# A perceiver's wide cross attention: order of TensorE's work in every second step, and of ScalarE's and VectorE's beside it

## What is computed

```python
def _L0_xattn_ref(x, context, ln_gamma, ln_beta, w_q, w_kv, w_out, b_out, gate):
    xn = _layernorm(x, ln_gamma, ln_beta)
    q = (xn @ w_q).reshape(B, SQ, NUM_HEADS, DIM_HEAD)
    kv = context @ w_kv
    k, v = jnp.split(kv, 2, axis=-1)
    k = k.reshape(B, SK, NUM_HEADS, DIM_HEAD)
    v = v.reshape(B, SK, NUM_HEADS, DIM_HEAD)
    scores = jnp.einsum('bqhd,bkhd->bhqk', q * SCALE, k)
    attn = jax.nn.softmax(scores, axis=-1)
    out = jnp.einsum('bhqk,bkhd->bqhd', attn, v).reshape(B, SQ, INNER)
    out = out @ w_out + b_out
    return out * jnp.tanh(gate[0])
```

## Time and profile before

| | |
|---|---|
| median of 3 runs | 4327.76 us (4327.47 to 4329.01) |
| the profiled execution | 4329.77 us |
| its span, first to last instruction | 4327.1 us |
| TensorE busy with matmuls | 3896.4 us (90% of the span) |
| VectorE, ScalarE, POOL busy | 2700.6, 2460.7, 1633.4 us |
| mean granted TensorE clock | 0.952 of full speed |
| DMA, mean over the span | 168 GB/s |

### The profile page before, as it was taken

How to read it: one execution, slowest core, us unless ns; L and a number is a source line. 1 busy time by engine, 2 the same in 40 slices (tenths; PEclk the granted TensorE clock), 3 DMA queues, 4 the chain that set the end, 5 groups by cost and what they waited for, 6 DMA issues and landing times. The chain is left out here.

```text
span 4327.1 us, 75594 instructions
## 1 busy us (share of the span) xinstructions
PE 3896.4 (90%) x27192; PEld 2768.8 (64%) x27192; DVE 2700.6 (62%) x4077; ACT 2460.7 (57%) x4518; POOL 1633.4 (38%) x1301
## 2 busy tenths in 40 slices
PE   5899999999999999999677985899999999967399
PEld 2677777777777777776445974555555555433288
DVE  5766666666666666664174213677777777658577
ACT  3577777777777777776142112455555556625165
POOL 1566666666666666666222002100000000014033
PEclk9999999999999999999797997999999999979699
DMA  5777777776777766663213566644444422100011
GB/s 200 269 253 250 245 255 253 250 255 240 265 252 250 247 238 224 228 226 118 65 20 120 197 230 209 191 147 138 143 147 140 137 69 66 34 23 1 12 50 42
DMA packets 232719, 724.99 MB, mean 168 GB/s; under 512 B 44556, under 2 KB 129804, under 8 KB 163724
## 3 DMA queue, kind: packets, MB, share of 16 engines
q1 hardware_dynamic: 229664, 711.78, 48.3%
q0 software_dynamic: 2688, 8.39, 0.5%
HBM read 625.70 MB, written 94.37 MB: 166 GB/s over the span
## 5 line engine op out<-in xcount | busy, mean ns | idle before, releaser
L752 POOL TENSOR_TENSOR wa_acc<-wa_acc,wa_probs 128x512 f32<-128x512 f32 x960 | 1246.4, 1298 | 526.8 <-ACT wa_probs L613 446.4
L677 DVE TENSOR_REDUCE wa_mx<-wa_ps_m 128x2 f32<-128x1024 f32 x512 | 626.8, 1224 | 486.5 <-PE wa_ps_m L488 486.3
L613 ACT ACTIVATE wa_probs<-wa_ps_s 128x512 f32<-128x512 f32 x1024 | 556.0, 595 | 528.9 <-PE wa_ps_s L534 523.6
L1204 ACT ACTIVATE na_probs<-na_ps_s 128x512 f32<-128x512 f32 x1024 | 564.2, 599 | 379.1 <-PE na_ps_s L1108 373.7
L1256 DVE TENSOR_REDUCE na_mx<-na_ps_m 128x1 f32<-128x512 f32 x1024 | 643.5, 682 | 187.7 <-PE na_ps_m L1093 186.7
L605 ACT ACTIVATE wa_ps_s<-wa_m_wide 128x512 f32<-128x512 f32 x1024 | 575.4, 605 | 1.0
L510 PE MATMUL wa_ps_o<-wa_probs,wa_values 128*64 128x256 f32 x4096 | 507.3, 390 | 0.0
L1093 PE MATMUL na_ps_m<-na_keys,na_q 98*128 98x512 f32 x1024 | 425.1, 423 | 43.6 <-DVE na_mx L1256 30.2
L1108 PE MATMUL na_ps_s<-na_q,na_keys 100*128 100x512 f32 x1024 | 430.4, 428 | 2.4 <-ACT na_probs L1204 1.5
L449 PE MATMUL wa_ps_k<-wa_k_ctx,wa_w_k 128*128 128x512 f32 x1488 | 388.3, 396 | 0.0
L475 PE MATMUL wa_ps_v<-wa_w_v,wa_v_ctx 128*128 128x256 f32 x2880 | 383.1, 282 | 0.0
(11 more groups left out here) (342 smaller groups left out, 5503.6 us busy)
## 6 DMA issues: line engine op xcount, KB each, us to landing
wa_k_ctx<-ctx_split SPq DMA_DIRECT2D x248, 1024.0 KB, 5.1
wa_v_ctx<-ctx_split SPq DMA_DIRECT2D x120, 1024.0 KB, 5.8
na_ctx<-ctx_split SPq DMA_DIRECT2D x56, 1024.0 KB, 6.9
na_keys<-k_rows SPq DMA_DIRECT2D x192, 256.0 KB
ctx_split<-wa_stage SPq DMA_DIRECT2D x32, 1024.0 KB, 9.1
wa_land<-in_ctxT SPq DMA_DIRECT2D x32, 512.0 KB, 9.9
ge_w_b<-in_w_rows SPq DMA_DIRECT2D x8, 2048.0 KB
k_rows<-na_k_high SPq DMA_DIRECT2D x64, 256.0 KB, 2.3
```

What stands on the lines that cost most here:

```text
L613: act.activation(probs[:, c % R:c % R + 2, h * SQ:(h + 1) * SQ], ps_s[n % BANKS][:, :].rearrange("p (c n) -> p c n", c=2), ACT.Exp).then_i ...
L677: dve.tensor_reduce(mx[:, half, :, k], ps_m[:, :, :], AX.X, ALU.max).then_inc(m_taken, 1)
L752: pool.tensor_tensor(acc[:, :], acc[:, :], probs[:, c % R, :], ALU.add).then_inc(summed, 1)
L1204: act.activation(probs[:, n % RP, :], ps_s[n % RS][:, :], ACT.Exp).then_inc(exp_done, 1)
```

## The change

In odd steps TensorE keeps its order. In even steps the value unit comes first, then the high products, which now open the sum, then the maximum, then the low products, which now close it and tell ScalarE of it (s_ready, one increment a head). The low products of an even step thus stand right before the weighing of the odd step behind. On ScalarE initial(2t+3) moves between the two exponentials, except at st 15. On VectorE the rest of the keys goes before the maximum.

```diff
@@ -518,22 +518,29 @@
                                     start=True, stop=True)
                 ins.then_inc(den_done, 1)
 
-            def scores(t):
+            def seeded(t):
+                if t % ST == 0:
+                    pe.wait_ge(kl_ready, 2 * CG * (t // ST + 1))
+                pe.wait_ge(init_done, 2 * t + 2)
+
+            def scores_low(t, last):
                 a, c = t // ST, t % ST * 2
-                n = 2 * t
-                if c == 0:
-                    pe.wait_ge(kl_ready, 2 * CG * (a + 1))
-                pe.wait_ge(init_done, n + 2)
                 for i in range(2):
                     for h in range(2):
                         r = slice(h * DH, (h + 1) * DH)
-                        pe.matmul(ps_s[(n + h) % BANKS][:, i * SQ:(i + 1) * SQ], keys[a % 2][h][r, (c + i) * P:(c + i + 1) * P],
-                                  ql[a % 3][r, :], start=False, stop=False, skip_group_check=True)
+                        ins = pe.matmul(ps_s[(2 * t + h) % BANKS][:, i * SQ:(i + 1) * SQ], keys[a % 2][h][r, (c + i) * P:(c + i + 1) * P],
+                                        ql[a % 3][r, :], start=False, stop=last, skip_group_check=True)
+                        if last and i:
+                            ins.then_inc(s_ready, 1)
+
+            def scores_high(t, last):
+                a, c = t // ST, t % ST * 2
                 for h in range(2):
                     for i in range(2):
-                        ins = pe.matmul(ps_s[(n + h) % BANKS][:, i * SQ:(i + 1) * SQ], keys[a % 2][h][:, (c + i) * P:(c + i + 1) * P],
-                                        qh[a % 3][:, h, :], start=False, stop=True, skip_group_check=True)
-                    ins.then_inc(s_ready, 1)
+                        ins = pe.matmul(ps_s[(2 * t + h) % BANKS][:, i * SQ:(i + 1) * SQ], keys[a % 2][h][:, (c + i) * P:(c + i + 1) * P],
+                                        qh[a % 3][:, h, :], start=False, stop=last, skip_group_check=True)
+                    if last:
+                        ins.then_inc(s_ready, 1)
 
             open_banks()
             for k in range(CG):
@@ -554,18 +561,29 @@
                 if st == 1 and t > 1:
                     denominator(a - 1)
                 unit = max_unit(t)
-                if t >= -1 and unit is not None:
-                    maximum(*unit)
-                if 0 <= t < LAST:
-                    scores(t)
-                if st == ST - 1 and a + 1 < G:
-                    turn_maximum(a + 1)
-                kb = key_block(t)
-                if kb is not None:
-                    project_keys(kb)
-                unit = value_unit(t)
-                if unit is not None:
-                    project_values(*unit, turns=(t + 1) // ST + 1)
+                values_unit = value_unit(t)
+                if t % 2:
+                    if t >= -1 and unit is not None:
+                        maximum(*unit)
+                    if 0 <= t < LAST:
+                        seeded(t)
+                        scores_low(t, False)
+                        scores_high(t, True)
+                    if st == ST - 1 and a + 1 < G:
+                        turn_maximum(a + 1)
+                    kb = key_block(t)
+                    if kb is not None:
+                        project_keys(kb)
+                if values_unit is not None:
+                    project_values(*values_unit, turns=(t + 1) // ST + 1)
+                if t % 2 == 0:
+                    if 0 <= t < LAST:
+                        seeded(t)
+                        scores_high(t, False)
+                    if t >= -1 and unit is not None:
+                        maximum(*unit)
+                    if 0 <= t < LAST:
+                        scores_low(t, True)
 
         @block.scalar
         def _(act):
@@ -626,16 +644,18 @@
                 kb = key_block(t - 1)
                 if kb is not None:
                     take_keys(kb)
+                ahead = st == ST - 1 and a + 1 < G
                 if t >= 0:
                     exponents(2 * t)
+                    if not ahead:
+                        initial(2 * t + 3)
                     exponents(2 * t + 1)
-                if st == ST - 1 and a + 1 < G:
+                if ahead:
                     take_maximum(a + 1)
                     initial(2 * t + 2)
-                if t >= -1:
                     initial(2 * t + 3)
-                    if st != ST - 2:
-                        initial(2 * t + 4)
+                if t >= -1 and st != ST - 2:
+                    initial(2 * t + 4)
                 if t >= 0 and st == 4 and a < BLOCKS - CG:
                     split(a + CG)
 
@@ -723,14 +743,14 @@
                     take_values(*unit)
                 if st == 1 and t > 1:
                     copy_out(a - 1)
+                kb = key_block(t - 1)
+                if kb is not None:
+                    take_keys(kb)
                 unit = max_unit(t)
                 if t >= -1 and unit is not None:
                     take_maximum(*unit)
                 if st == ST - 2 and 0 <= a < G - 1:
                     finish_maximum(a + 1)
-                kb = key_block(t - 1)
-                if kb is not None:
-                    take_keys(kb)
                 if t == LAST + 1 or (st == 3 and 1 <= a < G):
                     divide(a - 1)
                 if st == 5 and 0 <= a < BLOCKS - CG:
```

## The result

The changed kernel takes 4348.3 us (median of 5 runs, 4344.6 to 4351.0) against 4327.8: ratio 1.0047, 95% interval 1.0036 to 1.0058, so slower by 20 us. The profiled execution took 4349.35 around a span of 4346.7, 19.6 more than before.

The account below looks back on a forecast made before the run. The prediction took TensorE's queue length to bound the main stretch. Its terms, -48.5 + 33.3 + 26.0 + 2.4 + 2.3 - 4.2 + 6.2 - 1 = +16.5, on 4329.8 less 2.0 gave 4344 us, range 4320 to 4368.

Parts of the forecast that it names:

- Regrouping: TensorE's step pairs: four changes of array shape instead of five, 0.19 us saved in each of 255 pairs, -48.5.
- Two value units: Steps 43 to 46: the second value unit waits for VectorE's copy out of ps_v, 1.11 us each, +33.3.
- Keys before the maximum: Pairs without a value unit: VectorE's later maximum stalls TensorE 1.18 us, 22 times, +26.0.
- The steps of the splits: Where ScalarE also splits context, the chain to the next maximum misses by some 0.10 us, 23 times, +2.3.
- free by 0.4: Regular pairs: VectorE's maximum ends at 6.72 us, the next wants to start at 7.11, so no wait.
- Block edges: Low's wait for initial goes at 15 edges with values, -4.2 us; high waits longer at 15 without, +6.2.
- The last block: Earlier initial(2t+3) is worth 0.34 us each, but POOL's sums already take 5.57 a pair: -1 (0 to -3).
- A: Rival, faster: TensorE's change from low to weighing is free, another 38 us goes, 4306; chance 0.10.
- B: Rival, about the same: waits of terms 2 and 3 are 0.3 us shorter, 52 times, 4328; chance 0.15.
- D: Rival, slower: TensorE's change from low to weighing costs 0.20 us or more, +13, 4357; chance 0.05.
- E: Rival: no gain from grouping, as full-array matmuls' loads cannot run under the one before, 4392 us; chance 0.02.
- C: Rival, slower: the clock falls in the first block's pairs and some double-value pairs, 4354 to 4384 us; chance 0.12.

Follow-up runs that it names:

- e5: Changed kernel with ScalarE's and VectorE's orders as before, only TensorE's order changed; ratio 1.0162 to the kernel before, span 4398.8 us.
- e2: Changed kernel with TensorE projecting values before keys in odd steps that have a value unit; ratio 0.9975 to the kernel before, span 4317.5 us.
- e1: Changed kernel with the maximum before the keys on VectorE in even steps without a value unit; ratio 0.9989 to the kernel before, span 4318.5 us.
- e6: Changed kernel with TensorE's order as before, only ScalarE's and VectorE's orders changed; ratio 1.0074 to the kernel before, span 4359.1 us.
- e4: Changed kernel with ScalarE's order as before, both exponentials and then both initials; ratio 1.0062 to the kernel before, span 4347.1 us.
- e8: Changed kernel with the edits of e1 and e2, and the division's product moved from step 3 to step 7; ratio 0.9909, span 4287.3 us.
- e9: As e8, with TensorE's old order in step 0 of blocks without a value unit there; ratio 0.9908 to the kernel before, span 4288.3 us.
- e3: Changed kernel with VectorE's division in step 4, behind the maximum, instead of step 3; ratio 1.0134 to the kernel before, span 4378.6 us.

## Why the prediction was right, point by point

The forecast was 4344 with a range of 4320 to 4368 and "slower" at 0.67; measured are 4348.3.

1. *Regrouping* (-48.5): 0.200 a regular pair instead of 0.19, low to weighing 0.15 as taken. e5 shows that it comes from TensorE's order alone. No price of the second increment shows.
2. *Two value units* (+33.3): the wait is 0.92 net of the saving in 30 pairs, as forecast; e2 took it away and got 31.8 back.
3. *Keys before the maximum* (+26.0): the mechanism was right, and e1 and e6 show it; the size was 1.32 a wait instead of 1.18, because ScalarE's initial starts 0.09 behind the exponential that it waits for, not 0.03, twice before the keys. e4, without these waits, has it at some 0.6 (TensorE idle 0.53). It fell on 21 of the 22 pairs; the earliest waits only some 0.3.
   *The steps of the splits* (+2.3) failed. What made the next maximum late in the changed kernel is the division, in 30 pairs and by 0.33, 7 more than forecast. The step that failed is one that the forecast doesn't name: VectorE's division stands in front of the keys at step 3 and was put at nothing. With the product at its 0.47 of before it might have passed; on the new order it meets POOL's sum and takes 1.09. Odd blocks lost the delay in e1, where the product takes 0.43 again, even blocks in e8, where it is moved away. The room was also smaller than the forecast's "free by 0.4": with the 0.65 that it takes from a waiting maximum it is 0.25, which is why it could have the splits miss by 0.10. The split's own price is 0.25 and not 0.10; it shows in e1 in 12 odd blocks and in e8 in 11 even ones too, the 23 of the forecast, and is hidden behind the division's wait in the changed kernel.
4. *Block edges* (-4.2 and +6.2): -0.59 and +0.21 a pair against -0.47 and +0.22. The 0.10 set aside for the turning did not come in 14 of the 15 edges; in one it came as 1.25, when m_neg met a sum of POOL. e9 confirms the second.
5. *The last block* (-1) was mis-sized. POOL's sums were counted as a bound on each pair; they may run up to eight chunks behind (probs has eight places) and bind only at the end. The pairs fell to 5.30, TensorE idles 1.14 a pair instead of 1.44, and the clock stayed up in all but one of them, where before it was down in seven of nine: -10.1. Two pairs that ran at the full clock before gained 0.29 each, so of the 10.1 only some 2.6 (nine times 0.29) is the reordering itself, as against 2.7 in the forecast's column; the rest is the clock, whose gain the forecast has nowhere. POOL then took 3.4 of it back in the last denominator.

```profile
2093.18 11.18 POOL L772 TENSOR_TENSOR wa_acc<-wa_acc,wa_probs 128x512 f32<-128x512 f32 x8
```

```profile
2097.21 2.09 PE L510 MATMUL wa_ps_o<-wa_probs,wa_values 128*64 128x256 f32 x16
2104.41 1.12 PE L517 MATMUL wa_ps_o<-wa_acc,g_ones 128*64 128x256 f32 x4 [5.10 <-POOL wa_acc L772]
```

Errors 3 and 5 have opposite signs, +7 and -4, and with term 3's size leave 3 us in the profiled execution. That the forecast is only 4 off is in part luck; that it says "slower" is not, since the three large terms, -48.5, +33.3 and +26.0, came out at -51 (by 0.200 a pair), +33.5 and +28. Rivals A, B, D and E are out by the rows above: 0.15 at low to weighing, waits at or over their forecast, full-width groups still 0.12 a matmul. C did not happen where it was placed: the clock is 1.00 there.

## What to carry to other kernels

On an engine that is never idle, read the price of each change of the array's shape from the ends of neighbouring groups, and then write down for every moved piece which buffer's release now stands between two users: here one bank (ps_v) and one queue order (VectorE's) took back more than the 50 us that the grouping gains, and two small edits (e1, e2) repaired both. An order that is right for the long pairs can be wrong for the short ones, so each kind of period in the schedule needs its own sum. And an experiment that moves one engine's phase can change another engine's durations; look at the mean of a line before and after, not at its place alone. When a repair uncovers a new wait, look for a group of periods that has the suspect and not the wait: the blocks without a split of context cleared the product in e8.

## What the hardware showed that was not expected

**VectorE behind POOL.** Three of VectorE's instructions whose operands are all in SBUF end a fixed time behind the end of the sum that POOL was running when they started, and so whatever was left of it: the 128x256 product and m_neg, 0.43 long alone, 0.28 behind it, and the low part of the split, 1.23 long alone, 1.08 behind it. In both cases that is as if they began 0.15 before its end. The product takes 1.09 in the median of the changed kernel and 1.55 in e3, m_neg up to 1.48 in e4 and e5. The reciprocal, with one operand, took 1.75 each time, and the rest of the keys, with one operand in PSUM, 0.69, under a sum or not. The Trainium skill (SBUF — State Buffer, "SBUF: two separate sides") states that VectorE and GpSimd share a port pair as an exclusive lock for a whole instruction, with two SBUF inputs or in a two-port mode on VectorE's side; the durations agree with it. Whether m_neg, with one input, runs in such a mode no run here shows.

**The clock.** In e5 TensorE fell to 1.2 GHz behind 14 of 29 idle stretches of 1.85; behind idle stretches of 1.23, six in the changed kernel's first block, it did not. In the last block it was down in seven of nine pairs before, where most idle stretches are 1.44, and in one of nine behind the change, where most are 1.14.
